# First attention: the second group of transposes of a slot behind the slot's other products

## The reference, cut to what matters

```python
xqkv = x @ Wqkv                                  # 1024 x (16 + 2*4)*128
xq, xk = rope(xq), rope(xk)                      # v is left as it is
scores = einsum('bhsd,bhtd->bhst', q, k) * D**-0.5
mask = triu(full((S, S), MASK_NEG), 1)
probs = softmax(scores + mask, axis=-1)
att = einsum('bhst,bhtd->bshd', probs, v).reshape(B, S, H*D)
x = x + ga * (att @ Wo)
```

## Time and profile before

| | us |
|---|---|
| median of 3 runs | 783.2 |
| lowest and highest | 782.8, 784.45 |
| the profiled execution | 783.09 |
| its span | 781.3 |
| PE busy | 720.8 (92%) |
| DVE busy | 553.2 (71%) |
| ACT busy | 443.6 (57%) |
| POOL busy | 379.7 (49%) |

### The profile page before, as it was taken

The page is one execution under the profiler, slowest core; times in us unless marked ns, Lnnn a source line. Parts: engine busy times, 40 slices in busy tenths (PEclk is TensorE's granted clock), DMA queues, the critical chain, the costliest instruction groups (busy, mean ns, idle before and its releaser), DMA issues. The chain is left out here.

```text
span 781.3 us, 12361 instructions
## 1 busy us (share of the span) xinstructions
PE 720.8 (92%) x4372; PEld 622.1 (80%) x4372; DVE 553.2 (71%) x1257; ACT 443.6 (57%) x915; POOL 379.7 (49%) x410
## 2 busy tenths in 40 slices
PE   5797999999999999999999799999979999889997
PEld 4576888888888888888887689997768778567787
DVE  3466777677776776768777688777578888566666
ACT  3464666666666666666666343322678776546432
POOL 5792586536865368643451330002656554204773
PEclk9998999999999999999999999999999999999999
DMA  7000000000000000004000040003100000000001
GB/s 248 4 11 8 14 16 15 13 8 14 10 20 14 8 15 8 13 15 170 7 8 8 1 135 1 1 1 115 49 0 2 1 1 1 0 3 1 1 1 55
DMA packets 19083, 19.85 MB, mean 25 GB/s; under 512 B 2126, under 2 KB 16974, under 8 KB 19022
## 3 DMA queue, kind: packets, MB, share of 16 engines
q1 hardware_dynamic: 18206, 18.41, 7.4%
q10 hardware_dynamic: 816, 0.66, 0.3%
HBM read 18.01 MB, written 1.05 MB: 24 GB/s over the span
## 5 line engine op out<-in xcount | busy, mean ns | idle before, releaser
L880 POOL TENSOR_TENSOR at_swapped<-at_swapped,at_sin 128x512 f32<-128x512 f32 x40 | 51.6, 1289 | 134.3 <-ACT at_swapped L603 134.3
L625 ACT ACTIVATE at_probs<-at_probs,at_negmax 128x128 f32<-128x128 f32 (+7 forms) x128 | 99.6, 778 | 29.4 <-DVE at_negmax L709 27.5
L709 DVE CUSTOM_DVE_ANT_0 at_probs<-at_scores,causal 128x128 f32<-128x128 f32 (+7 forms) x128 | 96.2, 751 | 16.9 <-PE at_scores L59 16.2
L518 PE MATMUL at_turn<-ident_sb,at_probs 128*128 128x128 f32 x576 | 86.4, 278 | 15.0 <-DVE at_full_T_lo L725 13.9
L518 PEld LDWEIGHTS at_turn<-ident_sb,at_probs 128*128 128x128 f32 x576 | 67.5, 142 | 23.8 <-issue 11.7
L618 ACT ACTIVATE at_edge_T_hi<-at_turn 128x128 fp32r<-128x128 f32 (+3 forms) x128 | 55.5, 434 | 34.8 <-PE at_turn L518 34.4
L57 PE MATMUL at_scores<-at_kT_hi,room 128*128 128x512 f32 (+1 forms) x192 | 66.6, 347 | 4.5 <-DVE at_v L691 3.5
L618 ACT ACTIVATE at_full_T_hi<-at_turn 128x512 fp32r<-128x512 f32 x64 | 38.3, 598 | 50.4 <-PE at_turn L518 48.4
L58 PE MATMUL at_scores<-at_kT_lo,room 128*128 128x512 f32 (+1 forms) x192 | 66.7, 347 | 0.0
L59 PE MATMUL at_scores<-at_kT_hi,room 128*128 128x512 f32 (+1 forms) x192 | 66.4, 346 | 0.0
L725 DVE TENSOR_TENSOR at_edge_T_lo<-at_turn,at_edge_T_hi 128x128 fp32r<-128x128 f32 (+3 forms) x128 | 61.4, 480 | 1.4 <-ACT at_edge_T_hi L618 1.0
(11 more groups left out here) (395 smaller groups left out, 2289.9 us busy)
## 6 DMA issues: line engine op xcount, KB each, us to landing
at_wq_in<-L_attn_Wqkv SPq DMA_DIRECT2D x16, 128.0 KB, 2.2
at_wo_in<-L_attn_Wo SPq DMA_DIRECT2D x16, 128.0 KB, 2.0
staging<-L_ffn_routed_w SPq DMA_DIRECT2D x7, 256.0 KB, 4.7
ff_wmod<-L_wmod SPq DMA_DIRECT2D x1, 1536.0 KB, 6.5
at_wmod<-L_wmod SPq DMA_DIRECT2D x1, 1024.0 KB, 8.3
staging<-L_ffn_w_gate SPq DMA_DIRECT2D x1, 1024.0 KB, 5.2
staging<-L_ffn_w_up SPq DMA_DIRECT2D x1, 1024.0 KB, 7.3
staging<-L_ffn_w_down SPq DMA_DIRECT2D x1, 1024.0 KB, 9.7
```

The source lines that it names most:

```text
L518: mm = pe.transpose(p_turn[t % 2][:, b - b0, :], probs[:, s % 4, b * P:(b + 1) * P], m.ident[:, :])
L625: act.activation(row, row, ACT.Exp, scale=-1.0, bias=negmax[:, unit % 4:unit % 4 + 1], accum_out=rowsum[:, unit // NT % 2, i:i + 1])\
L709: dve.tensor_tensor_reduce(out=probs[:, s % 4, 0:width], in0=p_scores[s % 2][:, 0:width], in1=m.causal[:, S - width:], scale=-1.0, scalar= ...
L880: turning = pool.tensor_tensor(swapped[:, r % 2, :], swapped[:, r % 2, :], sin[:, cols], ALU.mult)
```

## The change

`turn` gets a parameter `part`, by which it issues one group alone. In a slot, group a stays where it was; group b, where there is one, is issued behind all other products of the slot. The calls of `turn` behind the last slot are as before. Only PE's program is touched.

```diff
-                def turn(unit):
+                def turn(unit, part=None):
+
                     g, s = divmod(unit, UNITS)
                     pe.wait_ge(exp_done, unit + 1)
                     for n, (b0, b1) in enumerate(blocks(s % NT)):
+                        if part not in (None, n):
+                            continue
                         t = g * PER_KV * TGROUPS + tgroups_before(s) + n
...
                     scores(g, h, i)
                     if unit < 4:
                         value_job(4 + unit)
+                    two = unit >= 2 and len(blocks((unit - 2) % NT)) == 2
                     if unit >= 2:
-                        turn(unit - 2)
+                        turn(unit - 2, 0)
...
                         out_job(head - 1, i - 4)
+                    if two:
+                        turn(unit - 2, 1)
```

## The result

| | before | changed |
|---|---|---|
| median, us | 783.83 (4 runs, 782.8 to 787.1) | 826.75 (4 runs, 826.28 to 827.44) |
| span of the profiled run, us | 781.3 | 824.6 |
| granted clock, mean | 0.991 | 0.989 |

The ratio is 1.0529, with a 95% interval of 1.0507 to 1.0551: 5.3% slower, which is 41.5 us of 783.8. The medians differ by 42.9 and the two profiled spans by 43.3, so the cost is known to some 2 us and no better. I had said 830, in a range of 818 to 852.

What follows compares the result with a forecast made beforehand. The prediction took TensorE to bound the stage, with ScalarE and VectorE close behind. Heads 1 to 13 cost 41.6 us, 14 and 15 4.3, head 0 0.9: 46.8 on 783.1 gave 830 us, 80% range 818 to 852.

Steps and rivals of the forecast that it cites:

- step 2: s0 to s2: 6b's late copy delays the query product's copy, 7b and the attention of s2; 0.94 us more a head.
- The two dearer kinds of head: Five heads with a key product in s1, three with s0's query product ahead of the scores: up to 0.4 us dearer.
- step 1: s6 to s0: 4b's late copy delays ScalarE's and VectorE's queues, the output product of s7 and 6a; 2.14 us a head.
- The moved instruction itself: TensorE's order alone, group b behind products four times a head: 0.4 us a head at most, taken as zero.
- A: Rival: faster or no slower, as banks are emptied behind products and transposes' waits go; 772 us; 3%.
- B: Rival: only step 1 costs time, since the query copy in s0 has enough room; 815 us; 10%.
- C: Rival: TensorE's clock falls in each of 13 heads, 2 us each, 26 us more; 856 us; 14%.

Runs made afterwards that it cites:

- late_s6: Against the kernel before: group b (4b, one transpose) issued late in s6 only; 815.03 us, ratio 1.0387.
- late_s0_s1: Against the kernel before: group b issued late in s0 and s1 only; 798.18 us, ratio 1.0158.
- s6_last: `late_s6` with 4b's copy behind the attention's copy on ScalarE and its lo part behind the attention's lo part on VectorE; 783.87 us, ratio 0.9991 to the kernel before.
- late_s7: Against the kernel before: group b (5b) issued late in s7 only; 784.73 us, ratio 1.0.
- s6_s7_last: Against the kernel before: group b late in s6 and s7, its copy and lo part also at the slot's end on ScalarE and VectorE; 795.95 us, ratio 1.0144.
- s6_s7_queues: ScalarE's and VectorE's queues as in `s6_s7_last`, TensorE's order as in the kernel before; 795.55 us, ratio 1.0142 to the kernel before.
- late_s6_s7: Against the kernel before: group b issued late in s6 and s7 only; 814.51 us, ratio 1.0378.
- all_last: Against the kernel before: group b at the slot's end on all three engines, in all four slots; 844.93 us, ratio 1.0771.

## Why the prediction was right

**The mechanism, point by point.** ScalarE waits in front of 4b's copy (2.08, said: some 2); the output product of s7 idles, ended by x, in 15 heads (1.55, said 1.9); 6a idles behind it (0.35, said 0.6); the query product's copy in s0 follows the exponential without a gap; s2 starts late because of 7a's bank and then 7b. `late_s6`, `late_s0_s1` and `s6_last` show it as cause, and not only as order in time. What the forecast calls step 2 was 0.94 and measured 0.90 in a head like the one above. The two dearer kinds of head are there too: 1.03 with a key product (6a to the attention of s2 207.40 to 215.20, before 192.10 to 198.87) and 1.14 with the query product ahead of the scores (262.57 to 269.37, before 241.72 to 247.38). Over the 13 heads that is 0.11 more in the mean, and I had taken 0.12, from 3.08 to 3.2.

**The term that was mis-sized** is step 1: 2.14 said, 1.82 measured. 0.07 of it is that 4b's copy began at 4.60 instead of 4.67. 0.11 is that the attention's copy came 1.20 behind that copy and not 1.31: in the changed kernel it begins at 231.06, while the exponential's last part runs from 230.97 for 0.19. 0.12 is that the maximum of s7 begins 0.78 behind the addition and not 0.90. The last 0.02 is in the other distances. The 0.12 has a likely reason in the trace of before, where the maximum began at 214.91 and this product of its scores ended at 214.88:

```profile
214.49 0.39 PE L59 MATMUL at_scores<-at_kT_hi,room 128*128 128x512 f32 x1
```

So I had probably carried a distance that held a wait for TensorE inside, and that wait was gone once the queue was late. The profile names no releaser for it, so this is argued and not shown.

**The sum with the measured terms.** 6a of head 1 to 6a of head 14 took 354.05 us (97.91 to 451.96) after 317.32 (94.02 to 411.34): 36.7 more, 2.83 for each of 13 heads where I had 3.2. Up to 6a of head 1 the stage lost 2.8 (head 0's step 2 and head 1's step 1), behind head 14 another 2.0. That is 41.5 for the stage, where I had 46.8. That it equals the 41.5 from the ratio is in part chance, for the two profiled spans differ by 43.3: 1.1 us lies ahead of the stage, where the clock was lower in this execution (0.80 and 0.52 in 35 to 45 us, before 0.97 and 0.68), and 0.7 behind it.

**The moved instruction itself** was rightly priced at nothing: the intervals of `late_s7` and `s6_last` hold 1 and reach 0.3% at most, and `s6_s7_last` and `s6_s7_queues` can't be told apart.

**The rivals.** A (faster) is out: the waits of the transposes stayed, 12.7 of 13.9. The Trainium skill has the rule behind it (Perfetto Trace Analysis, section Matmuls), that groups should rotate through banks so that the emptying of one overlaps the products of the next. Both kernels do so, and the wait in front of 6a is 0.35 after 0.37; what decided was what the emptying engines had queued behind. B (step 1 alone, 815) is out by `late_s0_s1`. C (the clock at each head) did not happen in the changed kernel's trace, and its four executions, 826.28 to 827.44, leave room for one fall of 1.5 us at most. But my reason for holding it unlikely was too weak, that the waits are shorter than 2.7: in `late_s6_s7`, with the same 1.55 in front of the output product, the clock fell in three heads. What C had too large is its size: a fall costs some 1.5 us, and it comes in few heads, not in 13. The Trainium skill (TensorE: Matmul & The Clock Gate, section HAM oscillation) has the clock fall at each repetition of an idle gap that is too long; the trace of `all_last` agrees for its waits of 3.85 or more, with 0.73 behind 3.86 us of idle, and for its waits of 2.19 the clock fell at three of five.

## What to carry to other kernels

Before moving an instruction later on the engine that is the bound, look at the engine that takes its result: if that engine serves in a fixed order, all that stands behind the result's reader moves too, however small the instruction (here one transpose of 0.3 us cost 1.8 us a head). Move the reader with it, or leave both; and ask who needs the buffer that the moved reader frees, which cost 11 us in `s6_s7_queues`. Compare the clock of two runs before a difference is explained by waits alone. When a distance between two rows is carried into a forecast, check that the later one wasn't waiting for something else.

## What was not expected of the hardware

Nothing in the changed kernel. In `all_last`, TensorE's clock fell behind single waits of 3.9 us in a stage that is otherwise some 90% busy (36.66 us of the 40 from 150 to 190) and came back (0.73, 0.93, 1.00 in stretches of 5 us from 225 on). And the same waits don't always do the same. In the changed kernel 1.55 and 0.35 in each head left the clock at 1.00 for 340 us, while in `late_s6_s7`, with the same two waits, it fell in three heads. No run here shows what makes the difference.
